# Constant biases instead of pointers, a second split of the normalizing step between GpSimd and ScalarE, and 56 of 64 row gathers issued inside the last batch

## What is computed

```python
def _ln_c(v, eps=1e-6):
    m = jnp.mean(v, axis=-1, keepdims=True)
    s = jnp.var(v, axis=-1, keepdims=True)
    return (v - m) / jnp.sqrt(s + eps)
...
x = x + _L0_conv_ref(_ln_c(x), ...)
t = _to_tokens(x)
t = t + _L0_ffn_ref(_ln_t(t), ...)
```

```python
logits = jnp.einsum('bsd,ed->bse', x, gate_w) + gate_b
probs = jax.nn.softmax(logits, axis=1)
vals, idx = jax.lax.top_k(probs.transpose(0, 2, 1), K)
...
gathered = jnp.take_along_axis(x, flat_idx[:, :, None], axis=1)
pooled = jnp.einsum('bked,bke->bed', gathered, topv)
h = jax.nn.gelu(jnp.einsum('ebd,edh->ebh', h, weight1), approximate=False)
out = jnp.einsum('ebh,eho->ebo', h, weight2)
outputs = outputs.at[jnp.arange(Bn)[:, None], flat_idx].add(weighted)
```

## Time and profile before

| | us |
|---|---|
| median of 3 runs | 2183.25 |
| lowest and highest | 2180.88, 2188.42 |
| the profiled execution | 2181.99 |
| its span in the profile | 2180.2 |

### The profile page before, as it was taken

One profiled execution on the slowest core, in us unless ns is written; L12 is line 12 of the kernel. 1 busy time (PEld: TensorE's weight loads), 2 busy tenths in 40 slices (PEclk: granted clock), 3 DMA queues, 4 the chain that ended last, 5 costly groups with the idle time before them and its releaser, 6 DMA issues.

```text
span 2180.2 us, 41787 instructions
## 1 busy us (share of the span) xinstructions
PE 1907.0 (87%) x11909; PEld 1280.9 (59%) x11909; DVE 1826.1 (84%) x4598; ACT 1879.7 (86%) x4808; POOL 1986.2 (91%) x2124
## 2 busy tenths in 40 slices
PE   6999999999999999999999999999999987634991
PEld 5866666666666666666666666666666632321561
DVE  4689899999999999999999999899999899621661
ACT  6999999999999999999999999999999988812420
POOL 5799999999999999999999999999999999464377
PEclk9999999999999999999999999999999999755995
DMA  5498888888888888888888888888888577953953
GB/s 191 153 260 215 222 224 230 203 225 221 226 210 224 221 227 223 226 218 216 225 220 226 211 226 221 225 223 229 213 220 219 150 188 191 254 142 107 267 89 32
DMA packets 111063, 447.88 MB, mean 205 GB/s; under 512 B 10575, under 2 KB 52404, under 8 KB 61684
## 3 DMA queue, kind: packets, MB, share of 16 engines
q1 hardware_dynamic: 81140, 302.61, 40.7%
q0 software_dynamic: 29696, 142.61, 36.5%
HBM read 306.78 MB, written 138.41 MB: 204 GB/s over the span
## 4 chain that ended last, share of the span: by engine, by line
POOL 48%; issue 20%; ACT 17%; PE 9%; DVE 4%; POOLq 1%; DMA 0%; another core or an unknown queue 0%; SPq 0%; ACTq 0%; DVEq 0%
POOL U L418 21%; POOL U L423 17%; ACT U L538 7%; POOL zn L439 5%; POOL U L430 3%; ACT zT L501 3%; ACT UT L495 2%; ACT LTS L510 2%; POOL out_dram L473 1%; PE G L733 1%; PE T L715 1%; PE O L788 1%; ACT LTS L565 1%; PE O L757 1%; POOL nA L403 1%
## 5 line engine op out<-in xcount | busy, mean ns | idle before, releaser
L538 ACT ACTIVATE U<-xa,nA,rA 128x128 f32<-128x128 f32 x1948 | 798.5, 481 | 0.6 <-issue 0.6
L733 PEld LDWEIGHTS G<-UT 128*128 128x128 f32 x4096 | 534.8, 192 | 231.2 <-issue 217.3
L418 POOL TENSOR_TENSOR U<-U,bet 128x512 f32<-128x512 f32 x512 | 652.6, 1275 | 3.5
L733 PE MATMUL G<-UT 128*128 128x128 f32 x4096 | 541.9, 275 | 0.3 <-DVE Gs L940 0.3
L423 POOL TENSOR_TENSOR U<-U,rO 128x512 f32<-128x512 f32 x512 | 532.9, 1041 | 3.5 <-ACT rO L519 3.5
L439 POOL TENSOR_TENSOR zn<-U,rZ 128x512 f32<-128x512 f32 x467 | 510.9, 1094 | 24.4 <-PE T L722 24.4
L666 PE MATMUL O<-U,MT 128*128 128x512 f32 x1024 | 528.3, 598 | 0.0
L935 DVE BATCH_NORM_STATS2 stA<-xa 128x6 f32<-128x256 f32 x1024 | 385.9, 424 | 69.9 <-POOL nA L405 41.5
L917 DVE BATCH_NORM_STATS2 stO<-O 128x6 f32<-128x256 f32 x1024 | 385.7, 421 | 34.0 <-PE O L666 32.7
L1013 DVE BATCH_NORM_STATS2 stZ<-U 128x6 f32<-128x256 f32 x1024 | 386.1, 422 | 12.7 <-DMA U<-in_x 12.6
L722 PE MATMUL T<-ident,zn 128*128 128x128 f32 x2048 | 327.6, 283 | 75.9 <-POOL zn L439 53.6
(11 more groups left out here) (152 smaller groups left out, 1644.0 us busy)
## 6 DMA issues: line engine op xcount, KB each, us to landing
xa<-in_x SPq DMA_DIRECT2D x128, 1024.0 KB, 5.9
U<-in_x POOLq DMA_DIRECT2D x128, 1024.0 KB, 8.2
out_dram<-U SPq DMA_DIRECT2D x128, 1024.0 KB, 7.0
U<-in_L_ffn_weight SPq DMA_DIRECT2D x112, 256.0 KB
LTS<-in_L_ffn_weight SPq DMA_DIRECT2D x16, 256.0 KB
xa<-out_dram,UT POOLq DMA_INDIRECT x64
out_dram<-U,UT POOLq DMA_INDIRECT x64
zT<-in_L_ffn_weight SPq DMA_DIRECT2D x1, 128.0 KB
```

The lines of the kernel that those rows point to most:

```text
L418: gp.tensor_tensor(rows(a, i), rows(a, i), bet_b, ALU.add).then_inc(S["gb"], 1)
L538: last = sc.activation(utile(a, i, j), xa[:, k % XR, h * W:(h + 1) * W], ACT.Identity, scale=rA[:, k % 2, h:h + 1], bias=nA[:, k % 2, h:h ...
L733: last = te.matmul(G[:, 0:P], v, v, start=(i == 0 and j == 0), stop=(i == NI - 1 and j == TI - 1))
```

## The change

All constants for the Ln's epsilon become numbers in the instruction, and the tile `eps` with its three memsets goes. The eviction of the logits becomes a plain copy, and the gate's bias is added in step 121 + 1 of a batch on DVE to the candidates' values (a tensor_scalar in place of a copy). In the batches before Z_ACT the z of items 3, 11 and 27 is made on ACT (43 items), and from item Z_ALL = 549 - 76 = 473 on every z is. `spread` and `places` are called three times: for batches 0 to 13 in steps 545 and 547, for batch 14 in steps 576 and 578, and for batch 15 behind the steps. The gathers of batches 0 to 13 stand one per step in steps 549 to 604, at the step's end; 8 are left behind the steps. Within them a gather's source is named as the part of `out` up to the batch that it may read.

```diff
+PARTS = ((545, 0, 14), (576, 14, 15))
+S_GATH = 549
...
+Z_ALL = S_GATH - L_ZN
+Z_ITEMS = (3, 11, 27)
...
-            return a[0] * NI + i >= Z_ACT and i % 4 != 3
+            n = a[0] * NI + i
+            return i in Z_ITEMS if n < Z_ACT else i % 4 != 3 or n >= Z_ALL
...
+            def gather(q, n):
+
+                gp.indirect_dma_start(out=R[:, q, n, :], out_offset=None, in_=rows_v[0:max(n + 1, NB - 2) * HW, :],
+                                      in_offset=bass.IndirectOffsetOnAxis(ap=idx[:, q, n:n + 1], axis=0),
+                                      ).then_inc(s_rows[q][n // 8], 16)
...
+                    g = b[0] * NI + t - S_GATH
+                    if 0 <= g < Q * (NB - 2):
+                        if g == 0:
+                            pool.wait_ge(R_["idx"], 1)
+
+                            for k in range(2 * NK):
+                                pool.wait_ge(s_store[k], 16 * (NB // 2 - 1))
+                        gather(*divmod(g, NB - 2))
...
-                        sc.activation(LTS[:, s % 2, o:o + IW], LT[:, :], ACT.Identity,
-                                      bias=gb2[:, 0:1]).then_inc(S["lt_done"], 1)
+                        sc.activation(LTS[:, s % 2, o:o + IW], LT[:, :], ACT.Copy).then_inc(S["lt_done"], 1)
...
-                        sc.activation(sO[:, :], stO[:, p % 2, :, 2], ACT.Ln, scale=1.0 / W, bias=eps[:, 1:2]).then_inc(S["o_ln"], 1)
+                        sc.activation(sO[:, :], stO[:, p % 2, :, 2], ACT.Ln, scale=1.0 / W, bias=EPS_O).then_inc(S["o_ln"], 1)
...
-                        wait(act, S["zn"], cnt(a, NI, i + 1 - 2 * NI))
+                        if a[0] >= 2:
+                            wait_zn(act, (a[0] - 2, None), i)
...
-                        ve.tensor_copy(XV[:, :, :], mv[:, :, 0:NS * K]).then_inc(S["xv"], 1)
+
+                        ve.tensor_scalar(XV[:, :, :], mv[:, :, 0:NS * K], gb2[:, 0:1], None, ALU.add).then_inc(S["xv"], 1)
```

63 lines of the change are left out of this document (28 added, 35 removed).

## The result

The changed kernel takes 2171.58 us (median of 7, 2165.46 to 2174.54); the kernel before takes 2185.11 beside it. The ratio of the two is 0.9937, interval 0.9927 to 0.9947: 13.7 us faster. The forecast was 42 to 44 us faster (2141, range 2108 to 2172). The profiled execution has a span of 2163.7 us against 2180.2, 16.5 less.

| stretch | forecast | in the trace |
|---|---|---|
| start to step 527 (1737.53, now 1724.80) | -21 | -12.7 |
| steps 527 to 574 (last beta 1869.10, now 1882.73) | +19 | +26.4 |
| to the first gather of the last batch (1930.3, now 1955.75) | +1 | +11.8 |
| from there to the first scatter (110.1 long, now 67.4) | -41 | -42.7 |
| first scatter to the end (139.9, now 140.6) | 0 | +0.7 |

A forecast was written before the change was run, and what follows sets the result against it. POOL was taken to set the steps' pace with ACT just behind, and gathers to stall the expert stage. Terms -21 + 19 + 1 - 41 = -42 gave 2141 us on the median's scale, range 2108 to 2172.

The forecast's parts named there:

- part 1: Steps 76 to 527: pointers go, 43 z move to ACT, period falls 1.5 us per batch: -21 us.
- part 2: Steps 549 to 574: a gather in each and no z on POOL, 3.41 us per step against 2.79: +19 us.
- part 3: Steps 575 to 605: four z on ACT, shorter places() wait, last 30 gathers through before the last index: +1 us.
- part 4: Expert stage: gather stream of 88 us shrinks to about 10, PE's gap mostly goes: -41 us.
- What bounds the kernel: POOL sets the steps' pace, ACT 1 us behind per batch; in the expert stage engines stand still beside gathers.
- "issue" and "remote": Expert stage: words naming no engine, read as instructions that arrive late beside the gathers; no size given.
- a short stream does no harm: From 1904 to 1921, beside the first gathers, DVE still ran 28 instructions; argument against the standstill moving into the steps.
- rival C: Standstill moves into the steps: 30 gathers hold ACT's z some 33 us, 26 single ones cost 32: 2206, chance 0.08.
- A: Expert stage: the standstill has another cause than the gathers and stays, so part 4 gives nothing: 2182, chance 0.11.
- B: Steps to 527: moved z delay ACT's Ln, Exp and U, POOL waits, part 1 is 0: 2162, chance 0.10.
- D: Steps: POOL's limits are real, ACT's waits shrink and a gather costs 0.60 us: 2108, chance 0.09.

The follow-up runs named there:

- e2_no_z_wait: Changed kernel without ACT's semaphore wait for z ahead of U: 2155.85 us on chip 1, ratio 0.9867 to the kernel before.
- e15_small_gap: Kernel before plus a 128x1 memset on POOL behind each gather: 2134.86 us on chip 2, ratio 1.0002.
- e14_steps_only: Kernel before with pointers gone, z items 3, 11 and 27 on ACT, no z wait ahead of U, gathers unmoved: 2109.69 us on chip 2.
- e13_steps_gap: e14_steps_only plus a 128x256 memset on POOL behind each gather: 2112.36 us on chip 2, ratio 0.9894 to the kernel before.
- e16_gap_again: Kernel before plus a 128x256 memset on POOL behind each gather: 2157.21 us on chip 12, ratio 0.9878.

## Why the prediction was wrong, point by point

The forecast was 42 us, the traces differ by 16.5. The 25.5 us between them are 8.3 in part 1, 7.4 in part 2, 10.8 in part 3, -1.7 in part 4 and 0.7 in the end. Three steps failed: the semaphore waits ahead of U, put at nothing; the slot of a gather, put at 0.95 us; and above all the 30 gathers in a row beside the z of ACT, which were to hold up nobody ("they are through before the last index is made") and cost ACT 16.6 us of standstill.

- **What bounds the kernel.** Right for the steps. For the expert stage the place and the trigger were right, the reading of "issue" and "remote" as late instructions stays open. The gathers were read as one stream of 88 us; they are rows of 15 and of 49, with a break of 7.5 us. The argument for "a short stream does no harm" (28 DVE instructions from 1904 to 1921) holds for some 12 gathers only: the last of these instructions starts at 1918.18, and then DVE stands still for 5.9 us.
- **Part 1, -21, measured -12.7.** The durations held within 4 ns. The term that failed is the one that was set to nothing: "The second semaphore that PE and ACT now wait on has been passed by then; its issue lies beside running work." ACT is full, with nothing to lie beside. Without both waits the period is 112.59 and step 527 comes 28.6 us earlier than before. The miss is larger than the total shows: the period fell by 0.47 us, where 1.5 was forecast, and 5.8 of the 12.7 us are gained before the third batch's first beta, with the waits or without (5.5 in e2_no_z_wait), which the sum had not told apart. The bounds (-42 to 0) held it.
- **Part 2, +19, measured +26.4.** Mechanism right, size off. The slot of a gather between computations was set at 0.95 with 1.25 as its bound. It is 1.00 us of issue and 0.16 of idle time; and behind an accumulate, two DMA issues in a row, the gather starts 1.32 us after the accumulate did (1813.95 to 1815.27), where a z started after 0.60 (1851.38 to 1851.98). The wait ahead of the first gather was 1.97 us (3 forecast). The Trainium skill, page "SBUF — State Buffer", section "Who interferes with whom", says that POOL is shut out for a whole DVE instruction while VectorE holds the ports that they share; the 26 gathers take 964 to 1101 ns, beside DVE instructions of up to 2.3 us, so the trace does not show that at this place.
- **Part 3, +1, measured +11.8.** The dense row of 30 in the change was long enough to bring its own standstill, 16.6 us on ACT. This is rival C in the one place where its condition held, with half of the 33 us that C gave to the row. In the 26 single gathers it is absent, as the forecast said. On chip 14, without it, the stretch from step 574 takes 54.1 us instead of 73.0; the kernel before takes 52.2 without (e15_small_gap) and 61.2 with the standstill of its first row. So the row of 30 costs 19 us, the old row of 15 had cost 9, and the remaining 2 stand against the +1 of the forecast.
- **Part 4, -41, measured -42.7.** Right in place and size, on a chip that has the standstill; that the first measurement fell on one was luck. On chips without it (2 and 14) the part is +3.
- **The rivals.** A was dismissed by "it ends with the last gather", and rightly for this chip. B and D are out: part 1 gained 12.7, and a gather cost more than its bound of 0.60, not less. But none of the rivals asked whether the standstill belongs to every chip. With it: -13.7; without it: +17.2. (The two traces of chips 14 and 2 are 21 us apart, 14 of them at step 574, but the profiled execution of e15_small_gap is 2 us under its median.)

So the result is the sum of three trades. The first part pays on every chip tried (11 to 13 us at step 527 on chips 12 and 14 and on the first one, 28.6 without the waits on chip 1; the whole of it 25 us on chip 2). Moving the gathers into the steps costs 26 us on both kinds of chip and buys 43 minus 12 us only on one kind.

**A version that beats both, on a chip without the standstill:** e14_steps_only on chip 2, 2109.69, where the kernel before takes 2134.81 and the changed one (chip 14) 2153.86. e13_steps_gap costs 2.7 us more there and has the pacing that was worth 25 us on chip 12. Neither was run on a chip with the standstill; the 25 us are what the same gap was worth to the kernel before (e16_gap_again).

**Open.** What the 1.40 us are. A backlog in something that gathers fill and that the engines' instructions pass is the reading that fits the late start, the late end and the common ticks; it was not shown what it is, nor why chips 1 and 12 have it and 2 and 14 do not. Neither was ACT's wait of 35 us explained. Every run on record has a span from its trace, so none tells whether the recording of the trace has a part in the standstill. Whether plain transfers, or gathers 1.6 us apart, would be free of it on chip 12 was not measured.

## What to carry to other kernels

- Before a term is built on idle time that no releaser explains, put a row of instructions that wait for nothing into it, and time the kernel on a second chip. It would have shown that some 40 of the 43 us of the expert stage belong to the chip (110.1 us against 69.6).
- On an engine that is full, semaphore waits that have long been passed still cost (40 ns for two). Look for waits that another one implies, before work is moved.
- Pacing can beat moving: a memset of 0.33 us between gathers won 25 us on the chip where the whole change, with 56 gathers moved, won 15 to 21. On a chip without the standstill it cost 6.

## What the runs showed of the hardware that I had not expected

- Two kinds of chips for one kernel: 2181 to 2185 us (chips 1 and 12, and the first one), 2135 to 2137 (chips 2 and 14), with step 574 of the kernel before alike within 1 us (its beta starts at 1868.85 on chip 12, at 1869.74 on chip 2 in e15_small_gap).
- On chips 1 and 12, beside indexed transfers issued every 1.25 us by POOL, DVE, ACT and PE are held up from some 12 to 21 gathers into a row (14 to 27 us) until 1.5 to 8 us behind its end. In rows of added instructions DVE and ACT then get about one per 1.40 us, at common instants, but ACT, after 35 us idle, ran 19 at full pace first. POOL keeps its pace.
- A gather costs POOL 0.94 us in a row of gathers, 1.00 between computations, and 0.16 to 0.30 of idle time ahead of it; a short memset fits into that idle time.
